# New instruction lists on all five queues, and nine products of zeros on TensorE ahead of the first scores

## The reference

```python
x = x + _L0_xcond_ref(_layernorm(x), ctx_2048, ctx_2048, itok_B_779_1933)
x = x + _L0_ffn_ref(_layernorm(x), w_router, w_fc, w_proj)
...
attn = jnp.einsum('bhdq,bhdk->bhqk', qh, kh)       # 8 heads of 16 features, 256 queries, 256 keys
attn = jax.nn.softmax(s * attn, axis=-1)           # s = SCALE * log(k_length), one per batch
out = jnp.einsum('bhqk,bhdk->bhdq', attn, vh)
...
h = jnp.einsum('nd,ehd->enh', x_flat, w_fc)        # 256 -> 1024, both experts
a = jnp.square(jnp.where(h >= 0, h, 0.5 * h))
expert_out = jnp.einsum('enh,edh->end', a, w_proj) # 1024 -> 256
out = jnp.einsum('end,en->nd', expert_out, mask * top_weight[None, :])
```

## Time and profile before

| | |
|---|---|
| median of 3 runs | 193.11 us |
| the profiled execution, its own time | 194.08 us |
| its span in the profile | 192.3 us |
| PE busy in the span | 159.3 us (83%) |
| DVE busy | 141.2 us (73%) |
| ACT busy | 97.6 us (51%) |
| POOL busy | 57.2 us (30%) |

### The profile page before, as it was taken

One profiled execution on the slowest core, in us unless ns is written; L12 is line 12 of the kernel. 1 busy time (PEld: TensorE's weight loads), 2 busy tenths in 40 slices (PEclk: granted clock), 3 DMA queues, 4 the chain that ended last, 5 costly groups with the idle time before them and its releaser, 6 DMA issues.

```text
span 192.3 us, 3953 instructions
## 1 busy us (share of the span) xinstructions
PE 159.3 (83%) x1440; PEld 135.2 (70%) x1440; DVE 141.2 (73%) x313; ACT 97.6 (51%) x179; POOL 57.2 (30%) x66
## 2 busy tenths in 40 slices
PE   0044797533899997999999989999999999999991
PEld 0033554312787685787899869997986999999991
DVE  5688954998789999999999999984278774141421
ACT  3402657943478574297437336562647344344520
POOL 6302354731040622210532402420223223244420
PEclk9999999995599999999999999999999999999999
DMA  4466999973000240421300420000010000010001
GB/s 123 168 221 193 261 309 338 263 248 108 0 31 27 78 143 27 159 65 53 114 2 29 143 78 5 27 2 3 0 55 3 0 0 3 0 55 3 0 0 55
DMA packets 18498, 16.31 MB, mean 85 GB/s; under 512 B 1840, under 2 KB 18352, under 8 KB 18480
## 3 DMA queue, kind: packets, MB, share of 16 engines
q1 hardware_dynamic: 17616, 15.28, 25.5%
q10 hardware_dynamic: 864, 0.79, 1.3%
HBM read 8.72 MB, written 1.05 MB: 51 GB/s over the span
## 4 chain that ended last, share of the span: by engine, by line
PE 51%; DVE 26%; issue 7%; SPq 5%; ACT 5%; DMA 4%; DVEq 0%; ACTq 0%
PE ops L1236 19%; PE hp L1218 18%; DVE negm L723 7%; PE pv L1202 5%; PE stp L1182 4%; DVE a_lo L821 3%; PE snp L1158 3%; DVE wproj_lo L843 2%; DMA cst<-consts 2%; DMA wfc_raw<-w_fc_t 2%; PE stp L1186 2%; ACT probs L436 2%; SPq L137 1%; SPq L168 1%; DVE pvt L742 1%
## 5 line engine op out<-in xcount | busy, mean ns | idle before, releaser
L322 POOL TENSOR_TENSOR a_buf<-l_buf 128x512 f32<-128x512 f32 x32 | 34.7, 1085 | 88.4 <-ACT l_buf L444 65.0
L821 DVE TENSOR_TENSOR a_lo<-a_buf,a_hi 128x512 fp32r<-128x512 f32 x32 | 23.1, 726 | 22.5 <-POOL a_buf L322 22.2
L436 ACT ACTIVATE probs<-stp 128x1024 f32<-128x1024 f32 x32 | 32.8, 1024 | 13.2 <-PE stp L1186 12.3
L1218 PE MATMUL hp<-xt_hi,wfc_hi 128*128 128x256 f32 x128 | 38.6, 301 | 0.4 <-issue 0.4
L1218 PE MATMUL hp<-xt_lo,wfc_hi 128*128 128x256 f32 x128 | 36.5, 285 | 0.0
L1218 PE MATMUL hp<-xt_hi,wfc_lo 128*128 128x256 f32 x128 | 36.4, 285 | 0.0
L723 DVE TENSOR_REDUCE negm<-snp 128x4 f32<-128x1024 f32 x28 | 34.1, 1219 | 3.1 <-PE snp L1158 3.0
L444 ACT ACTIVATE l_buf<-hp 128x512 f32<-128x512 f32 x32 | 19.1, 597 | 33.4 <-PE hp L1218 33.0
L1158 PE MATMUL snp<-k_st,q_st 64*128 64x256 f32 x112 | 14.9, 349 | 20.3 <-DMA q_st<-q_lo 10.8
L1236 PE MATMUL ops<-wproj_hi,a_hi 128*128 128x256 f32 x128 | 27.3, 294 | 0.0
L1218 PEld LDWEIGHTS hp<-xt_hi,wfc_hi 128*128 128x128 f32 x128 | 24.8, 193 | 3.0 <-issue 1.7
(11 more groups left out here) (73 smaller groups left out, 220.9 us busy)
## 6 DMA issues: line engine op xcount, KB each, us to landing
k_st<-k_hi SPq DMA_DIRECT2D x16, 128.0 KB, 2.1
wfc_raw<-w_fc_t SPq DMA_DIRECT2D x8, 256.0 KB, 5.4
wproj_raw<-w_proj_t SPq DMA_DIRECT2D x8, 256.0 KB, 5.2
q_st<-q_hi SPq DMA_DIRECT2D x14, 128.0 KB, 2.3
x_raw<-x SPq DMA_DIRECT2D x8, 128.0 KB, 2.9
k_st<-k_lo SPq DMA_DIRECT2D x8, 128.0 KB, 2.1
q_st<-q_lo SPq DMA_DIRECT2D x8, 128.0 KB, 2.1
v_raw<-ctx_t SPq DMA_DIRECT2D x8, 128.0 KB, 2.5
```

Source lines behind the costliest of these rows:

```text
L322: pool.tensor_tensor(a_buf[d % 2][:, :, :], l_buf[d % 2][:, :, :], l_buf[d % 2][:, :, :], ALU.mult).then_inc(s_a, 1)
L436: act.activation(probs[g][:, :, :, :], stp[:, :, :].rearrange("p e (c n) -> p e c n", c=KC), ACT.Exp).then_inc(s_exp, 1)
L821: dve.tensor_tensor(a_lo[d % NA][:, :, :], a_buf[d % 2][:, :, :], a_hi[d % NA][:, :, :].bitcast(f32), ALU.subtract).then_inc(s_alo, 1)
L1218: last = pe.matmul(hp[:, d % 2, half], wfc[w][:, kc, c * P:(c + 1) * P], xt[:, kc, :], start=(c % 2 == 0 and kc == 0 and w == 0 and xt is ...
```

## The change

Four things are in it. The lists on all five queues are new orders of nearly the same calls. On SP the first weight pieces go out between the stack DMAs of batches 0 and 1, where before all eight pieces of the first matrix went out in one run after them. DVE clears a new tile `blank` (128x256) and PE makes nine f32 products of it into the bank `ops`, before its first scores. One wait is added: `q_normalise(b)` waits for `q_part_lo(b-2)`, since lists may now run the normalisation earlier.

```diff
+        blank = sb("blank", [P, DIM])
...
+        s_blank = sem("blank_zeroed")
...
             def q_normalise(b):
                 j = b % 2
                 dve.wait_ge(s_xsc, b + 1)
+                wait(dve, s_qlo, b - 1)
...
+            def zero_blank():
+                dve.memset(blank[:, :], 0.0).then_inc(s_blank, 1)
...
             zero_q(0)
             zero_q(1)
+            zero_blank()
             x_moments(0, 0)
...
+            def warm(k):
+
+                if k == 0:
+                    pe.wait_ge(s_blank, 1)
+                pe.matmul(ops_[:, 0:DIM], blank[:, 0:P], blank[:, :], start=True, stop=True, skip_group_check=True)
...
+            warm(0)
+            warm(1)
+            warm(2)
+            warm(3)
+            warm(4)
+            warm(5)
+            warm(6)
+            warm(7)
+            warm(8)
             scores_qk(0, 0)
```

More of the change, by code:

```diff
@@ L905, in _ @@
             x2_moments(0, 1)
-            x2_moments(0, 2)
-            q_part_lo(3)
+            row_max(2, 0)
+            q_normalise(4)
+            x_moments(5, 0)
+            row_max(2, 1)
+            x_moments(5, 1)
+            x2_moments(0, 2)
+            x_moments(5, 2)
+            row_max(2, 2)
+            pv_turn(1)
+            row_max(2, 3)
+            den_inverse(1)
+            split_max_hi(2)
             x2_newton(0, 0)
+            split_max_lo(2)
+            attention_out(1)
@@ L941, in _ @@
[L941 to L947 removed]
+            x2_moments(1, 1)
+            x_newton(5, 1)
+            x2_moments(1, 2)
+            row_max(3, 0)
+            x2_newton(1, 0)
+            x_moments(6, 0)
+            x2_newton(1, 1)
+            x_newton(5, 2)
+            x2_newton(1, 2)
+            x_moments(6, 1)
+            x2_normalise(1)
@@ L1121, in _ @@
             x2_normalise(7)
+            square_lo(2, 3)
+            square_lo(2, 4)
+            xt_part_lo(3)
+            expert_out(2, 0)
+            router(6)
+            square_lo(2, 5)
+            square_lo(2, 6)
             router(7)
@@ L1333, in _ @@
             values(4, 0)
             values(4, 1)
-            max_transpose(5)
             ffn1(1, 0)
             ffn1(1, 1)
-            scores_kq(5, 0)
+            ffn1(1, 2)
             ffn2(0, 8)
-            scores_qk(6, 0)
-            scores_kq(5, 1)
+            max_transpose(5)
+            ffn1(1, 3)
             ffn2(0, 9)
             ffn2(0, 10)
+            scores_qk(6, 0)
+            scores_kq(5, 0)
+            ffn1(1, 4)
             ffn2(0, 11)
+            scores_kq(5, 1)
@@ L1388, in _ @@
             ffn2(1, 10)
+            scores_kq(6, 2)
+            scores_qk(7, 2)
+            x_transpose(2)
+            ffn2(1, 11)
+            scores_kq(6, 3)
             scores_qk(7, 3)
-            scores_kq(6, 3)
+            ffn2(1, 12)
             values(6, 0)
-            ffn2(1, 11)
+            values(6, 1)
+            ffn1(2, 0)
             max_transpose(7)
-            ffn1(2, 0)
-            ffn2(1, 12)
+            ffn1(2, 1)
             ffn2(1, 13)
+            ffn1(2, 2)
```

823 lines of the change are left out of this document (392 added, 431 removed).

## The result

The changed kernel takes 184.27 us (median of 4 runs, 184.18 to 187.47), and the kernel before, run beside it, 193.26 us (median of 4, 193.11 to 194.19). The ratio is 0.9524, with a 95% interval of 0.9485 to 0.9562: faster by 9.0 us. The forecast was 185.4, with a range of 181.5 to 190.0. The profiled execution took 184.18 us with a span of 182.4, against a span of 192.3 before, so it is 9.9 us shorter by the profile.

A forecast was written before the change was run, and what follows sets the result against it. PE was taken to bound 53.11 to 188.26: 188.3 - 2.0 - 3.8 - 3.1 + 0.2 + 1.0 = 180.6, plus a 4.04 us tail, 184.6 of span. That is 7.7 less, so 193.11 becomes 185.4 us; range 181.5 to 190.

The forecast's parts named there:

- `x_transpose(0)` starts earlier: End of the early stage: PE starts the first x2 transposes at 45.0 against 46.99, 2.0 us earlier.
- less left behind it: Behind `x_transpose(0)`: four `scores_qk`, three `scores_kq` and one `max_transpose` already done where PE was idle, 3.8 us less.
- the low clock behind it: Behind `x_transpose(0)`: 6.19 us of PE work ran at the low level before; half of it, 3.1 us, is saved.
- waits of PE behind it: Under "What is lost", behind `x_transpose(0)`: 0.2 us added for waits on `xt_part_lo(0)` and `row_max`, 1.0 for new orders interlocking worse.
- The nine products: PE's start: zeros from 3.3, done between 5.2 and 11.7, likely about 10.5; they cost 0, at most 0.9 us.
- The walk up to `x_transpose(0)`: Early stage by rows at high clock: exp(0, 0) at 18.4, exp(1, 3) at 34.4, `values(1, 1)` ending 35.5, then 9.4 of DVE.
- I take it as kept: High clock before 45: PE's longest idle time is 2.3 us, against the 6.12 that preceded the low level, so it stays high.
- the signs named ahead: Expected in the profile: `values(0, 0)` 1.0 us, `x_transpose(0)` near 45, no 0.50 clock near it, PE idle under 4 us behind.
- Rival (b): Clock low after all where the feed-forward starts; 3.1 us and 1.5 of early gain come back: 188.5 to 190; chance 0.18.
- Rival (d): Batches 2 to 7: PE stands 0.45 us at each of 24 `row_max`, 10.8 us lost: 195.2, slower; chance 0.10.
- Weights between the stacks: SP, batch 1: weights ahead of stacks; the last lands after 2.1 us at no cost, or after 5.4, costing 2.5.
- Rival (c): Stacks of batches 1 and 2 land late, `x_transpose(0)` starts 2 to 4 us later: 187.4 to 189.4; chance 0.12.

The follow-up runs named there:

- runs 7 and 8: Both on one chip: first the changed kernel again, 184.70 us (ratio 0.9482); then the changed kernel without the nine products of zeros, 186.82 us (0.9601).
- run 11: Changed kernel with 29 extra products of zeros in PE's gaps over both parts of the early stage: 181.86 us, ratio 0.9360.
- run 4: Changed kernel with the first three weight pieces on SP behind batch 1's last k stack, splits moved later: 185.30 us, ratio 0.9456.
- runs 3 and 11: Changed kernel with extra products of zeros in PE's early gaps: nineteen, 181.43 us (ratio 0.9327), and 29, 181.86 us (0.9360).
- 9 and 10: Changed kernel with extra products of zeros: nine ahead of `values(0, 1)` only, 183.30 us (0.9433); ten behind it only, 184.81 us (0.9523).
- run 5: Changed kernel's lists up to `x_transpose(0)` on every queue, remaining calls in the old kernel's order: 192.24 us, ratio 0.9892.
- run 6: Old lists up to `x_transpose(0)` with the nine products of zeros, the new order behind it: 201.08 us, ratio 1.0352.
- run 12: Changed kernel with an extra, unread 128x512 product of spare tiles on GpSimd behind each of 32 `square` calls: median 188.78 us.

## Why the prediction was right, and where it wasn't

The time was right, and so was the main mechanism: batch 2's attention now fills the time for which PE stood, less is left behind `x_transpose(0)`, and DVE's lists keep up. The sizes of the terms were partly wrong, and the errors cancelled. On the profiled spans, predicted and measured:

| term | predicted | measured |
|---|---|---|
| `x_transpose(0)` starts earlier | -2.0 | -0.4 (46.99 to 46.57) |
| less left behind it | -3.8 | -4.2 |
| the low clock behind it | -3.1 | -0.3 |
| waits of PE behind it | +1.2 | -3.2 (3.22 to 0.04 idle) |
| not in any of these, mostly steps between products | | -1.8 |
| sum | -7.7 | -9.9 |

The second measured row is what `scores_qk`, `scores_kq` and `max_transpose` take behind `x_transpose(0)` by the starts of neighbouring PE records (24.4 us before, 20.1 now), with the low clock taken off; the third is half the difference of PE's work there at the low level (5.8 and 5.1 us).

**The nine products.** Right that they cost nothing: they ended at 9.43 (predicted 10.5, bounds 5.2 to 11.7), and PE then waited 1.27 us for the q stack anyway. Their price of 0.93 us each at the low level was near: by the starts of neighbouring records it is 0.85 there and 0.43 at the high level, which came at 7.3, so nine took 6.10 us. Right too that they are worth something, which the clock column of the kernel before denied: 2.1 us by runs 7 and 8.

**The walk up to `x_transpose(0)`.** The first exp came at 18.76 (18.4), the last of batch 1 at 34.99 (34.4). That is luck in part: the walk took the high level all the way, and PE was at the low level from 14.1 to 21 and from 24.4 to 27.8 us. (A slip beside it: 10.84 to 32.96 holds five `scores_kq` and not six, so its price at the high level is 9.1 us; the pitch says the same.) Then DVE, the changed kernel in order of time:

```profile
37.49 0.70 DVE L748 STREAM_TRANSPOSE pvt<-pv 128x512 f32<-128x512 f32 x1
...
44.96 0.41 DVE L785 TENSOR_SCALAR x2n<-x,ymv,ysc 128x256 f32<-128x256 f32 x1
```

and PE:

```profile
35.80 0.50 PE L1165 MATMUL snp<-k_st,q_st 64*128 64x256 f32 x4 [0.85 <-DVE negm L729]
36.23 1.07 PE L1209 MATMUL pv<-probs,v_one 128*32 128x256 f32 x16
...
44.99 0.58 PE L1189 MATMUL stp<-q_st,k_st 64*128 64x256 f32 x2 [1.12 <-ACT probs L438]
...
46.01 0.63 PE L1165 MATMUL snp<-k_st,q_st 64*128 64x256 f32 x4
```

`values(1, 1)` stood behind `scores_qk(2, 2)`, which waited for a `row_max`, so the chain of batch 1 began at 37.49 and not at 35.5; it was shorter than my 9.4 us, and its last result is there at 45.37, against the 44.9 of the walk. What the walk left out is PE's own list: `scores_kq(2, 2)` waits for an exp until 44.99, and it and `scores_qk(3, 1)` run at the low level, which puts `x_transpose(0)` at 46.57. With the clock high the same pieces put it at 45.86 (run 11).

**"I take it as kept" was wrong.** The step read the clock by PE's longest idle time: 6.12 us had brought it down, so 2.3 us would not. It fell with no such idle stretch: just behind 14.0, with no wait of PE over 1.27 us between the zeros and there, near 24.4, behind waits of 0.87 and 0.89 us, and again between 41 and 42, behind waits of 1.74 us and less. So two of the signs named ahead failed: `values(0, 0)` took 1.93 us and not 1.0, and the column reads 0.50 around `x_transpose(0)`. Rival (b), the low clock there after all, happened nearly in full: 0.58 in 46.57 to 52.70, against 0.50 in the earlier trace rows, though the first `ffn1` itself was at the high level again. I had given it 0.18 and priced it at 188.5 to 190. That the time came out 4 us below is luck as far as the clock goes: the waits came out 4.4 us better than forecast, and the steps between products (below) brought time that was in no term. The Trainium skill ("TensorE: Matmul & The Clock Gate", "What's actually happening") says that a monitor sets the clock by how busy PE has been; run 11, with fillers in the gaps and 1.00 throughout, agrees, and so do the falls behind several short waits. My reading by the longest idle stretch alone did not follow from it.

**The low clock sets the spread between runs.** The time behind `x_transpose(0)` hardly varies: 135.8, 135.2 (run 7), 134.6 and 135.2 (without zeros), 135.4 (run 4), 134.3 and 134.2 (runs 3 and 11), 134.6 and 134.5 (9 and 10). What varies is its start: 46.57, 49.67, 46.80, 48.05, 50.14, 46.25, 45.86, 47.80, 47.94. In run 7, one kernel on one chip, the time is 183.66 us at a granted clock of 0.953, 186.71 at 0.922 and 187.70 at 0.914. With the clock held high (11) it is earliest and the runs agree. So the high level is worth some 2.5 us in all (184.3 or 184.7 to 181.9), about 1.5 of them behind the start (135.8 to 134.2) and the rest ahead of it. My 3.1 stood for an effect that the change itself did not bring, and it is twice what the high level brought behind the start.

**"What is lost": wrong in sign.** I added 1.2 us for waits; PE lost all but 0.04 us of its 3.22. Rival (d), 24 waits for `row_max`, did not occur. The waits of the changed kernel, us in total, times, longest:

```profile
DVE negm L729 <- PE snp L1165: 17.0, 19, 2.7
...
PE snp L1165 <- DVE negm L729: 2.3, 3, 1.1
```

It is DVE that waits for scores now (17.0 us, and 3.0 in the kernel before), as the count of work between the transposes had it. That the late order does this is shown by run 5 against the changed kernel: 140.4 against 135.8 behind `x_transpose(0)`, 4.6 us. Not all of that is waits: 2.5 us are PE's idle time, and about 0.5 are the clock (6.1 us of PE's work behind the start ran at the low level in run 5, 5.1 in the changed kernel); the other 1.6 are longer steps between products. The other 4.9 us (145.3 to 140.4) come with the new early half alone, which leaves less behind it and was priced at 3.8. By run 6 the halves can't be had apart: the late one without the early one costs 7 us.

**The 1.8 us more** were in no term. From the start of `x_transpose(0)` to PE's last product there are 9.5 us less (188.26 - 46.99 = 141.27 against 178.36 - 46.57 = 131.79), and the other terms explain 7.7. It is no idle time, and no record is missing: 1268 records start there before and 1226 now, and the 42 fewer are those of the blocks that moved. Most of it lies where PE goes from a feed-forward product to an attention product or back. The kernel before, PE in order of time:

```profile
59.95 0.39 PE L1218 MATMUL hp<-xt_hi,wfc_hi 128*128 128x256 f32 x1
60.17 0.28 PE L1218 MATMUL hp<-xt_hi,wfc_lo 128*128 128x256 f32 x1
...
60.52 0.28 PE L1218 MATMUL hp<-xt_hi,wfc_lo 128*128 128x256 f32 x1
60.64 0.28 PE L1218 MATMUL hp<-xt_lo,wfc_hi 128*128 128x256 f32 x1
60.85 0.39 PE L1182 MATMUL stp<-q_st,k_st 64*128 64x256 f32 x2
```

Between feed-forward products the starts lie 0.12 us apart, but 0.22 behind the first one and 0.21 ahead of the first attention product. Behind `x_transpose(0)` there are 69 such steps before and 61 in the changed kernel, which takes the attention products in longer runs; what they take over 0.12 each is 6.9 and 5.3 us in all, some 0.4 of the difference by the low clock. What is left, about 0.6 us, stays open, and so does why such a step costs more.

**Weights between the stacks.** Nothing that run 4 can tell, though its interval is wide (0.9324 to 0.9589), and the stacks land in 2.2 us. Rival (c), over 3 us of waits for stacks after 20 us, did not occur: they are 0.79 us.

## What to carry to other kernels

When a bound engine waits at one place for another engine's list, look for work of a later stage that both lists can do ahead of it, and move it on all queues together: half of such a move can cost more (201.1 us) than leaving it (194.1 on the same chip). Where two kinds of products share PE's list, count the places at which it goes from one to the other: here each costs about 0.1 us more than a step between equal ones. Whether PE keeps its high clock through a stage of many short waits can't be read from the longest wait; products of zeros in the waits settle it cheaply, as long as each fits in the wait. And when runs of one kernel scatter and those of another don't, look at the start of the stage that follows the thin one before explaining the medians.

## What the hardware showed that I had not expected

**Some DVE instructions grow while GpSimd works, and the other way round.** DVE lost 14.6 us of busy time with the same instructions; their lengths add up to 8.8 us less (152.1 to 143.3), and the rest is that neighbouring records overlap more. Against the median length of its own group (line, tiles, shape), 22 in the kernel before are over 0.2 us longer, 11.9 us in all, each begun while a GpSimd instruction ran; in the changed kernel 8, by 3.8 us; in run 12, 27, by 19.3 us. The kernel before, DVE in order of time, and under it POOL:

```profile
38.51 1.30 DVE L779 TENSOR_SCALAR x2n<-x,ymv,ysc 128x256 f32<-128x256 f32 x1
```

```profile
38.37 1.29 POOL L315 TENSOR_TENSOR wfc_lo<-wfc_raw,wfc_hi 128x512 fp32r<-128x512 f32 x1
```

`x2_normalise` takes 0.40 us otherwise; here it ends at 39.81, 0.15 behind the GpSimd instruction. Run 12 has both engines in a stream, DVE in order of time:

```profile
87.48 0.68 DVE L855 TENSOR_TENSOR wproj_lo<-wproj_raw,wproj_hi 128x512 fp32r<-128x512 f32 x1
88.08 1.53 DVE L833 TENSOR_TENSOR a_lo<-a_buf,a_hi 128x512 fp32r<-128x512 f32 x1
89.53 1.52 DVE L855 TENSOR_TENSOR wproj_lo<-wproj_raw,wproj_hi 128x512 fp32r<-128x512 f32 x1
90.97 1.21 DVE L735 TENSOR_REDUCE negm<-snp 128x4 f32<-128x1024 f32 x1
```

and POOL:

```profile
87.70 1.36 POOL L326 TENSOR_TENSOR a_buf<-l_buf 128x512 f32<-128x512 f32 x1 [4.92 <-DVE a_lo L833]
89.02 1.48 POOL L329 TENSOR_TENSOR spare<-spare 128x512 f32<-128x512 f32 x1
90.47 1.48 POOL L326 TENSOR_TENSOR a_buf<-l_buf 128x512 f32<-128x512 f32 x1
91.91 1.04 POOL L329 TENSOR_TENSOR spare<-spare 128x512 f32<-128x512 f32 x1
```

They take turns: `a_lo` at 88.08 ends at 89.61, 0.55 behind the POOL instruction that ended at 89.06; the next POOL one ends at 90.50, 0.89 behind that; and `wproj_lo` at 91.05, 0.55 behind that. Each alone takes 0.68 and 1.04. The `row_max` at 90.97, which reads scores from PSUM, keeps its 1.21 us though POOL is at work. It isn't alone: of the DVE instructions that began while a GpSimd product ran, 24 grew and 28 did not in the kernel before (counted against the lower quartile of their group), 8 and 39 in the changed one; maxima, transposes, statistics and reciprocals were not among those that grew. The Trainium skill ("SBUF — State Buffer", "SBUF: two separate sides") calls the port pair that GpSimd shares with DVE instructions of certain kinds an exclusive lock, held for a whole instruction; the trace agrees. In this kernel DVE was not the bound behind `x_transpose(0)`, so its 14.6 us are no term of the sum; whether they helped some of the waits there was not separated. Run 12 bounds it from the other side: 17 us more of DVE's time went with 1.2 us more behind `x_transpose(0)`.

**The clock fell without a long wait.** From 9.43 to 14.1 the changed kernel's PE waited 1.27, 1.08 and 0.63 us, and the granted clock went from 1.00 to 0.50. In 28 to 41 us, with waits up to 1.74 us and 7.88 us of work in 13.00, it stayed at 1.00.
